# Attention stage of a fused vision block: mask and row maximum as one VectorE operation per head, and weighing placed next to the scores

## The reference

```python
q = q * cos + _rotate_half(q) * sin
k = k * cos + _rotate_half(k) * sin
scores = jnp.einsum('bhgtd,bhkd->bhgtk', qg, k) / math.sqrt(DH)
scores = jnp.where(causal[None, None, None], scores, jnp.finfo(jnp.float32).min)
attn = jax.nn.softmax(scores, axis=-1)
ctx = jnp.einsum('bhgtk,bhkd->bhgtd', attn, v)
h = h + ctx @ Wo.T
```

## Time and profile before

| | us |
|---|---|
| median of three runs | 1462.11 |
| profiled execution | 1465.43 |
| its span, first to last instruction | 1463.4 |
| TensorE matmul busy | 1405.8 (96%) |
| VectorE busy | 1164.7 (80%) |
| GpSimd busy | 918.8 (63%) |
| ScalarE busy | 725.4 (50%) |
| L1401 mask, 256 times | 169.0, mean 660 ns |
| L1410 row maximum, 256 times | 176.2, mean 688 ns |

### The profile page before, as it was taken

How to read it: one execution, slowest core, us unless ns; L and a number is a source line. 1 busy time by engine, 2 the same in 40 slices (tenths; PEclk the granted TensorE clock), 3 DMA queues, 4 the chain that set the end, 5 groups by cost and what they waited for, 6 DMA issues and landing times.

```text
span 1463.4 us, 34061 instructions
## 1 busy us (share of the span) xinstructions
PE 1405.8 (96%) x10403; PEld 1100.7 (75%) x10434; DVE 1164.7 (80%) x2285; ACT 725.4 (50%) x2675; POOL 918.8 (63%) x958
## 2 busy tenths in 40 slices
PE   6999889999999999999999999789999999999997
PEld 3999767777777777777777777677677777777775
DVE  8988678889999999999999999776865655556565
ACT  6996566666766767676667667561100000000000
POOL 6895156767676767676676767345655556564653
PEclk8999999999999999999999999989999999999999
DMA  9456666777777777777777776868434344443432
GB/s 240 118 141 156 185 148 184 197 188 210 206 200 214 197 212 198 204 206 204 203 202 210 205 212 184 263 201 218 138 121 142 119 132 125 125 136 115 137 105 77
DMA packets 263401, 255.33 MB, mean 174 GB/s; under 512 B 72273, under 2 KB 200530, under 8 KB 263346
## 3 DMA queue, kind: packets, MB, share of 16 engines
q1 hardware_dynamic: 253394, 233.21, 57.5%
q10 hardware_dynamic: 9952, 21.43, 4.9%
HBM read 138.26 MB, written 106.57 MB: 167 GB/s over the span
## 4 chain that ended last, share of the span: by engine, by line
PE 72%; DVE 8%; POOL 6%; DMA 4%; SPq 3%; issue 3%; ACT 3%; ACTq 0%; DVEq 0%; POOLq 0%
PE att_ps L1101 30%; PE ffn_o L1777 22%; PE ffn_y L1881 6%; PE att_ps L1146 4%; PE att_ps L1160 4%; POOL yb L357 3%; SPq L877 2%; DMA p_blocks<-pB 2%; PE att_ps L1125 2%; POOL yb L363 2%; PE att_ps L1135 2%; PE mix_ps L446 1%; POOL pr L982 1%; DVE pB L1394 1%; DVE m L642 1%
## 5 line engine op out<-in xcount | busy, mean ns | idle before, releaser
L1232 ACT ACTIVATE pr<-sm,ml 128x128 f32<-128x128 f32 x1024 | 399.2, 392 | 224.4 <-DVE ml L1410 223.8
L982 POOL TENSOR_TENSOR pr<-pr,ri 128x512 f32<-128x512 f32 x256 | 265.4, 1041 | 135.2 <-DVE ri L1417 127.9
L1101 PE MATMUL att_ps<-w_hi,xT_hi 128*128 128x512 f32 x776 | 317.7, 409 | 2.6 <-DVE xT_lo L1358 1.9
L1101 PE MATMUL att_ps<-w_lo,xT_hi 128*128 128x512 f32 x776 | 315.6, 407 | 0.0
L1101 PE MATMUL att_ps<-w_hi,xT_lo 128*128 128x512 f32 x776 | 306.3, 395 | 0.0
L1777 PE MATMUL ffn_o<-wo_hi,cT_hi 128*128 128x512 f32 x528 | 212.5, 402 | 2.0 <-ACT wo_hi L1815 1.4
L1831 ACT CAST cT_hi<-ctx_in 128x512 fp32r<-128x512 f32 x64 | 36.3, 617 | 349.1 <-PE ffn_o L1777 346.1
L1777 PE MATMUL ffn_o<-wo_hi,cT_lo 128*128 128x512 f32 x528 | 206.4, 391 | 0.0
L1777 PE MATMUL ffn_o<-wo_lo,cT_hi 128*128 128x512 f32 x528 | 206.1, 390 | 0.0
L1394 DVE STREAM_TRANSPOSE pB<-pr 128x512 f32<-128x512 f32 x256 | 177.7, 694 | 34.3 <-DMA p_blocks<-pB 22.1
L1232 ACT ACTIVATION_READ_ACCUMULATOR pr<-sm,ml 128x1 f32 x1024 | 193.1, 189 | 0.0
(11 more groups left out here) (219 smaller groups left out, 2326.4 us busy)
## 6 DMA issues: line engine op xcount, KB each, us to landing
pT<-p_blocks SPq DMA_DIRECT2D x256, 256.0 KB, 2.9
p_blocks<-pB SPq DMA_DIRECT2D x512, 64.0 KB, 2.0
h_rows<-ho SPq DMA_DIRECT2D x64, 256.0 KB, 4.3
ctx_turned<-ctxo SPq DMA_DIRECT2D x64, 256.0 KB, 3.1
h_in<-h_rows SPq DMA_DIRECT2D x32, 512.0 KB, 3.7
out_dram<-yo SPq DMA_DIRECT2D x32, 512.0 KB, 2.6
ctx_in<-ctx_turned SPq DMA_DIRECT2D x30, 512.0 KB, 3.3
hbuf<-h_rows ACTq DMA_DIRECT2D x29, 512.0 KB, 4.0
```

The lines of the kernel that those rows point to most:

```text
L982: G.tensor_tensor(pr[:, g % 4], pr[:, g % 4], ri[:, g % 2, :].unsqueeze(2).to_broadcast([P, GQ, P]), ALU.mult).then_inc(p_ready, 1)
L1101: mm = nc.tensor.matmul(bank[:], x_part[:, t[1], e, tok:tok + P], w_part[blk][:, e, :], start=(r == 0), stop=(r == EC * 3 - 1))
L1232: a = nc.scalar.activation(pr[:, g % 4, q, :], sm[:, g % 2, q, :], ACT.Exp, bias=ml[:, b[1], 0, h:h + 1], accum_out=ml[:, b[1], 1, h:h + 1])
```

## The change

- `mask` and `row_maximum` become one function. For each of the group's four heads one `tensor_tensor_reduce` on 128x128 adds the mask to the scores, multiplies by -1, writes the negated scores to `sm`, and gives their minimum, which is the negated row maximum, to `ml`. A memset of one column of a small tensor `gates` stands in front of the four. The semaphore `negmax_ready` is gone; `masked` is now signalled after the fourth head, and ScalarE waits for it. ScalarE's exponential takes the scale -1.
- `weigh` moves from steps 3 and 7 to step 5 (right behind `scores(b, 1)`) and step 1 of the next turn (right behind `scores(b, 0)`), and `context`, `save_ctx` and `store` move with it: `save_ctx` to steps 6 and 2, `store` likewise. In the last turns (`weighed_late` is false from turn 31 on) the old order stays.
- `whole_p` runs at lag 6 in place of 5, except for the last two tiles. The DRAM tensor of the blocks has two copies, for even and odd tiles, and `part_p` waits for `weighed` in front of the last of its four transfers for groups 2 and 6. The blocks that the causal mask makes zero are filled in both copies, with six transfers in place of three.
- `split_x(n, 1)` in step 7 comes behind the mask on VectorE. `turn_q(b, 0)` waits for the first split of the next rows, not for both.

```diff
@@ -764,6 +763,10 @@
+    def weighed_late(t):
+        return not (fixed(t) and number(t) >= NB - 1)
     def rounds_at(t, s):
@@ -865,16 +868,21 @@
             sp.wait_ge(c_end_zero, 1)
-            for k, q in ((2, 0), (3, 0), (3, 1)):
-                sp.dma_start(p_dram[:, DH * k:DH * (k + 1), q, :].rearrange("g k f -> k g f"),
-                             c_end[DH * k:DH * (k + 1)]).then_inc(no_keys, 16)
+            for copy in range(2):
+                for k, q in ((2, 0), (3, 0), (3, 1)):
+                    sp.dma_start(p_dram[copy, :, DH * k:DH * (k + 1), q, :].rearrange("g k f -> k g f"),
+                                 c_end[DH * k:DH * (k + 1)]).then_inc(no_keys, 16)
 ...
             for q in range(4):
+                if q == 3 and g == 2:
+                    at_least(sp, weighed, 2 * number(b) - 1)
+                if q == 3 and g == 6:
+                    at_least(sp, weighed, 2 * number(b))
                 keys = min(q + 2, 4)
-                sp.dma_start(p_dram[g].rearrange("(k d) q f -> q d k f", k=4)[q, :, 0:keys],
+                sp.dma_start(p_dram[b[1], g].rearrange("(k d) q f -> q d k f", k=4)[q, :, 0:keys],
                              pB[DH * q:DH * (q + 1), g % 2, 0:keys].rearrange("d k h f -> d k (h f)")
@@ -882,13 +890,13 @@
                 sp.wait_ge(quantised, EC)
-                sp.wait_ge(no_keys, 48)
+                sp.wait_ge(no_keys, 96)
             sp.wait_ge(p_parted[g % 2], 256 * number(b) + 64 * (g // 2) + 64)
-            sp.dma_start(pT[:, g // 4, g % 4, :], p_dram[g].rearrange("k q f -> k (q f)")
+            sp.dma_start(pT[:, g // 4, g % 4, :], p_dram[b[1], g].rearrange("k q f -> k (q f)")
                          ).then_inc(p_whole[g // 4], 16)
         def body(t):
-            c = shifted(t, -2)
+            b, c = shifted(t, -1), shifted(t, -2)
             if exists(shifted(t, 2), NB) and fixed(t) and number(t) <= 0:
@@ -917,17 +925,22 @@
             for s in range(STEPS):
-                if s == 4 and exists(c, NB):
+                if s == 4 and not weighed_late(t) and exists(c, NB):
                     store(c, 0)
 ...
                     part_p(d, g)
+                d, g = group_at(t, s, 6)
+                if exists(d, NB) and not (fixed(d) and number(d) >= NB - 2):
+                    whole_p(d, g)
                 d, g = group_at(t, s, 5)
-                if exists(d, NB):
+                if exists(d, NB) and fixed(d) and number(d) >= NB - 2:
                     whole_p(d, g)
 ...
                     store_ml(c)
-                if s == 0 and exists(shifted(t, -3), NB):
+                if s == 6 and weighed_late(t) and exists(c, NB):
+                    store(c, 0)
+                if s == (2 if weighed_late(b) else 0) and exists(shifted(t, -3), NB):
                     store(shifted(t, -3), 1)
@@ -1028,8 +1041,10 @@
                     rope_sum(t, 0)
-                if s == 4 and exists(c, NB):
+                if s == (6 if weighed_late(t) else 4) and exists(c, NB):
                     save_ctx(c, 0)
+                if s == 2 and weighed_late(b) and exists(shifted(t, -3), NB):
+                    save_ctx(shifted(t, -3), 1)
                 if s == 1 and exists(b, NB):
@@ -1038,7 +1053,7 @@
                     rope_sum(t, 1)
-                if s == 7 and exists(c, NB) and not at(c, NB - 1):
+                if s == 7 and not weighed_late(t) and exists(c, NB) and not at(c, NB - 1):
                     save_ctx(c, 1)
@@ -1118,7 +1133,7 @@
                 if exists(shifted(b, 1), NB):
-                    pe.wait_ge(x_lo, 2 * nth(b) + 4)
+                    pe.wait_ge(x_lo, 2 * nth(b) + 3)
             else:
@@ -1171,6 +1186,10 @@
                     scores(b, s // 4)
+                if s == 1 and weighed_late(b) and exists(shifted(t, -3), NB):
+                    weigh(shifted(t, -3), 1)
+                if s == 5 and weighed_late(t) and exists(c, NB):
+                    weigh(c, 0)
                 if s == 5 and exists(t, NB):
@@ -1179,7 +1198,7 @@
                     turn_q(b, 1)
-                if s == 3 and exists(c, NB):
+                if s == 3 and not weighed_late(t) and exists(c, NB):
                     weigh(c, 0)
@@ -1194,7 +1213,7 @@
                     turn_x(n, 1)
-                if s == 7 and exists(c, NB):
+                if s == 7 and not weighed_late(t) and exists(c, NB):
                     weigh(c, 1)
@@ -1225,11 +1244,11 @@
             n = STEPS * number(b) + g
-            act.wait_ge(negmax_ready, n + 1)
+            act.wait_ge(masked, n + 1)
             at_least(act, p_turned, n - 3)
 ...
                 h = 16 * (g // 4) + 4 * q + g % 4
-                a = nc.scalar.activation(pr[:, g % 4, q, :], sm[:, g % 2, q, :], ACT.Exp,
+                a = nc.scalar.activation(pr[:, g % 4, q, :], sm[:, g % 2, q, :], ACT.Exp, scale=-1.0,
                                          bias=ml[:, b[1], 0, h:h + 1], accum_out=ml[:, b[1], 1, h:h + 1])
@@ -1283,7 +1302,9 @@
                     store_q(b, 1)
-                if s == 3 and exists(c, NB):
+                if s == 1 and weighed_late(b) and exists(shifted(t, -3), NB):
+                    context(shifted(t, -3), 1)
+                if s == (5 if weighed_late(t) else 3) and exists(c, NB):
                     context(c, 0)
@@ -1398,17 +1419,16 @@
             at_least(v, exp_done, n - 1)
-            V.tensor_tensor(sm[:, g % 2], S_BANK[g % 4][:].rearrange("p (q k) -> p q k", q=GQ),
-                            cst[:, C_MASK:C_MASK + P].unsqueeze(1).to_broadcast([P, GQ, P]),
-                            ALU.add).then_inc(masked, 1)
-        def row_maximum(b, g):
-            n = STEPS * number(b) + g
             if g == 0 and (not fixed(b) or number(b) >= 2):
                 v.wait_ge(ml_stored[b[1]], 16 * b[0])
-            v.wait_ge(masked, n + 1)
-            V.tensor_reduce(ml[:, b[1], 0, heads_of(g)], sm[:, g % 2], AX.X, ALU.max, negate=True
-                            ).then_inc(negmax_ready, 1)
+            V.memset(gates[:, g:g + 1], 0.0)
+            for q in range(GQ):
+                h = 16 * (g // 4) + 4 * q + g % 4
+                last = V.tensor_tensor_reduce(sm[:, g % 2, q], S_BANK[g % 4][:, q * P:(q + 1) * P],
+                                              cst[:, C_MASK:C_MASK + P], -1.0, 3.0e38, ALU.add, ALU.min,
+                                              ml[:, b[1], 0, h:h + 1])
+            last.then_inc(masked, 1)
@@ -1438,12 +1458,11 @@
                     split_x(n, 0)
-                    if x_steps(n)[1] is None:
-                        split_x(n, 1)
                 d, g = group_at(t, s, 1)
 ...
                     mask(d, g)
-                    row_maximum(d, g)
+                if s == 7 and x_steps(n)[1] is None and has_rows(n):
+                    split_x(n, 1)
                 if s == 0 and has_rows(b) and not last_rows(b):
@@ program @@
-    p_dram = nc.dram_tensor("p_blocks", (HKV, P, 4, P), F32, kind="Internal").ap()
+    p_dram = nc.dram_tensor("p_blocks", (2, HKV, P, 4, P), F32, kind="Internal").ap()
```

More of the change, by code:

```diff
@@ L689, in attention_stage @@
     pB, v_new = sbuf["pB"], sbuf["v_new"]
-    ml, ri, st, mv, ve, rstd, gate, wmax, wsc, winv = small_sb
+    ml, ri, st, mv, ve, rstd, gate, wmax, wsc, winv, gates = small_sb
     ps = [psum[f"att_ps{i}"] for i in range(8)]
@@ L745, in attention_stage @@
     masked = shared["masked"]
-    negmax_ready = sem("negmax_ready")
     exp_done = sem("exp_done")
@@ L2119, in program @@
         att_small = (sb("ml", (2, 2, HEADS)), sb("ri", (2, GQ)), sb("st", (2, 6)), sb("mv", (2,)), sb("ve", (1,)),
-                     sb("rstd", (1,)), sb("gate", (1,)), sb("wmax", (EC,)), sb("wsc", (EC,)), sb("winv", (EC,)))
+                     sb("rstd", (1,)), sb("gate", (1,)), sb("wmax", (EC,)), sb("wsc", (EC,)), sb("winv", (EC,)), sb("gates", (HKV,)))
         ffn_small = (sb("ffn_st", (2, 6)), sb("ffn_mv", (2,)), sb("ffn_ve", (1,)), sb("ffn_rstd", (1,)),
```

## The result

The changed kernel takes 1468.09 us (median of 7 runs, 1465.82 to 1472.59), the kernel before beside it 1461.79 (7 runs): a ratio of 1.0047 with a 95% interval of 1.0035 to 1.0059. It is 6.3 us slower, where 1454 and faster was forecast. The profiled execution took 1468.62 us, its span is 1466.8, against 1465.43 and 1463.4 before.

The account below looks back on a forecast made before the run. TensorE was taken to bound the kernel, busy throughout the 23.70 us steady turn. 1465.43 - 6.5 - 2 + 0.5 = 1457.4 us profiled, 3.3 less for the median: 1454.1 us; own range 1448 to 1459, wide range 1446 to 1471.

Parts of the forecast that it names:

- Part 1: Weighing next to scores on TensorE: saves 0.27 us per turn (0.03 to 0.37), 6.5 us over 24 turns.
- Part 2: Fused mask and row maximum on VectorE: 1.22 us per group (0.80 to 1.80) against 1.29, fitting without a wait.
- (a): VectorE's fused operation is dearer, over 1.29 us per group; at 1.5 the time is 1478 us; chance 0.20.
- (b): Gain and late mask signal cancel, group about 1.34 us or dearer steps into weighing: 1460 to 1462 us; chance 0.13.
- Part 3: Probabilities through DRAM on SyncE's queue: later loads and waits cost nothing, extra fills once 0.5 us (0 to 3.1).
- (c): SyncE's queue: later loads or fills meet crowded start or end, 3 to 5 us slower, 1457 to 1460; chance 0.08.
- the ring: Not forecast; follow-up theory of a 24 us loop: late transpose, late queue, last transfer behind the load, late transpose.
- Part 4: Early and last turns: the early ones gain 2 us (0 to 4), the last 0 (-3 to +3).
- the free step into weighing: Sign on TensorE: from the last score matmul to the first of the weighing no more than 0.25 us.
- the shorter wait of GpSimd: Sign: GpSimd's long wait for the context copy, 3.5 us per turn before, gets shorter.
- a SyncE queue that never waits for the weighing: Sign: if SyncE's queue stands waiting for the weighing, Part 3 is wrong.
- The steady turn of 23.4: Sign: steady attention turn at 23.4 us, TensorE busy throughout, no idle time in front of the second scores.

Follow-up runs that it names:

- e1: The changed kernel with ScalarE's 512 KB load of the rows of tile t+2 issued in step 1 instead of step 0: 1450.81 us, ratio 0.9913.
- e4: The changed kernel with the old two operations for mask and row maximum in place of the fused one: 1456.50 us, ratio 0.9956.
- e11: The kernel before with only the two DRAM copies, their six fills, later block loads and the waits for the weighing: 1465.52 us, ratio 1.0023.
- e3: The kernel before with the fused mask and minimum alone: 1460.80 us, ratio 0.9989.

## Why the prediction was wrong

By the spans the forecast was -6.5 us in the steady turns, -2 in the early ones, +0.5 for the fills and 0 at the end. Measured were +2.4, -0.9, +1.5 (the first scores come that much later) and +0.4; with the load late (e1) -9.0, -5.3, +1.5 and +0.4.

**Part 1** was right in kind and too small. The saving is (568.80 - 559.84) / 24 = 0.373 us per turn, the upper bound, where 0.27 was taken: both steps from scores into weighing cost nothing. 9.0 us over the 24 turns where the loop runs free (e1, e4).

**Part 2**: the term was mis-sized on the safe side, 0.85 us for a group instead of 1.22, below all but the lowest bound (0.80). Rivals (a) and (b), given a third of the chances for this, fell. The estimate of 1.34 us that was worked out from the Trainium skill (VectorE: DVE Perf Modes, section on the TRN2 errata) was 0.49 above what the trace shows.

**Part 3 is the step that failed**, with the sentence in Part 2 that ScalarE's context copies "move with the weighing" and its idle time covers them. SyncE's queue was costed by its free time, 2.75 us per turn, and by the count of what it issues, and found to cost nothing. Two questions weren't asked: what the context copy held back when it stood in step 7 (the 512 KB load behind it), and how much later the queue may run before its last transfer falls behind that load. The margins in the trace of before were there to be read: the part at -5.78 or -5.35, the load at -2.00, so the last transfer was out 1.8 to 2.5 us ahead of it. The landing itself, 5.14 us instead of 2.0, was in no row of the steady part, but rival (c) named it for the crowded ends ("a part's landing already stops VectorE") and gave it 0.08. In the steady part the ring costs 571.15 - 559.84 = 11.3 us, which is more than part 1 gives. The fills, 0.5 us, were too small as well: part 3 alone costs 3.9 (e11), of which the profiled executions show 1.7 in front of the first scores.

That 1468.09 still lies in the wide range up to 1471 is luck: that end was there for rival (a), a dearer fused operation, and the fused operation was cheaper than taken.

**Part 4**: the early turns were to gain 2 us. They gained 0.9 with the ring and 5.3 without it (e1). The last turn lost 3.2. Two parts land there late, one in 6.4 us beside the 512 KB loads of the feed-forward stage, one in 7.6 us behind a 1024 KB load of the output weights. But from the first scores of turn 31 to the end of the kernel it is 541.1 us before and 541.4 after: the 3.2 are made good behind the last turn, and the 0 that was taken for the end is right within its bounds. Other kernels with the new order took from 34.7 to 41.0 us there, and e3, with the old one, 38.1; what sets it stays open.

Of the signs named in advance, the free step into weighing came true in the changed kernel, and so did the shorter wait of GpSimd (83.7 us in the steady turns before, none after), the missing wait for the split of x in the early turns, and a SyncE queue that never waits for the weighing. This last one was to tell whether part 3 holds, and it could not see what went wrong there. The fused operations stand 0.21 us apart, below the 0.28 to 0.30 named. The steady turn of 23.4 came true in e1, not in the changed kernel; "more than 0.1 us there released by VectorE is rival (a)" was misleading, since VectorE was the releaser and a transfer in front of it the cause.

The best version is e1: the change, and the load one step later, 0.87% faster than before.

## What to carry to other kernels

When work is moved off a queue or an engine, look at what stood behind it there: a transfer that was held back by chance starts earlier, and what matters is which transfers it now overtakes. For a small transfer that something waits for, note by how many tenths of a microsecond it is issued ahead of the large ones, and how far the change can shift either. Here 0.3 us ahead was enough and 0.2 was not, and the change used up a margin of 1.8 to 2.5 us that no count of busy time shows. And when two edits do no harm alone and lose together, look for what they bring together before giving up either; here one load moved by a step settled it.

## What was not expected of the hardware

- A 64 KB transfer issued 0.2 us behind a 512 KB load on another queue landed in 5.14 us, against a median of 2.0. Issued 0.28 us or more ahead of the load, such transfers landed in at most 2.32 us, and so did those issued 2.1 us or more behind it. At the end of attention a part landed in 6.4 us beside three 512 KB loads, another in 7.6 us behind a 1024 KB load.
- The fused operation has an accumulator read of its own, 0.08 us, that starts with the next operation and costs nothing: 0.21 us from start to start for 128x128 from PSUM with a reduced value.
- The weighing (128 rows) follows the scores (32 rows) without a gap: 1.10 us from start to start for 32 matmuls, and the whole saving of the steady turn, 0.373 us, leaves nothing for this step.
